# Finer steps in the hand-written engine orders of a Flowformer layer with a routed MoE behind it

## The chip, the cores and the metric

The kernel runs on one core of a Trainium2 chip. The metric is the device time of one execution in microseconds (us), lower is better. Engines are named PE (TensorE), DVE (VectorE), ACT (ScalarE), POOL (GpSimd) and SP (SyncE, which issues most transfers).

## The reference, cut to what matters

Four sequences of 1,024 tokens with 256 features pass through one decoder layer (attention without a softmax, post-norm, a GELU network of width 1,024), a norm, and then a mixture of eight experts of width 1,024, each token to one expert, with a norm behind it.

```python
q, k, v = sigmoid(heads(Wq, bq)), sigmoid(heads(Wk, bk)), heads(Wv, bv)
sink_in = normal / sum(q * cumsum(k)); src_out = normal / sum(k * cumsum(q))
cons_sink = sum(q * cumsum(k * src_out)) / normal
cons_src = exp(clip(sum(k * cumsum(q * sink_in)) / normal))
src_comp = cons_src / cumsum(cons_src) * normal
kv = cumsum(einsum('bhld,bhlm->bhldm', k, v * src_comp))
x = einsum('bhld,bhldm->bhlm', q * sink_in / normal, kv) * sigmoid(cons_sink)
h = layernorm(inputs + x @ Wo + bo)
x = layernorm(inputs + layernorm(h + gelu(h @ W1 + b1) @ W2 + b2))
e = argmax(x @ router_w.T)
out = layernorm(x + square(relu(x @ fc[e])) @ proj[e])
```

## The kernel before

All data are 32-bit floats. The 4,096 tokens are cut into eight groups of 512 (G = 8), each of four chunks of 128 (NC = 4). A group passes through five stages, each one period later than the one before it (`LAG`): stage a (projections to k, q, v, running sums, the flow's normalisers), stage p (attention inside a chunk, the running state across chunks, product with Wo, first norm), stage b (turn of the normed rows, FFN up and down), stage c (second and third norm, router), stage d (place of each row in its expert's list, scatter to DRAM). In period n the engines work on stage a of group n, p of n-1, b of n-2, c of n-3 and d of n-4. Nine periods (0 to 8) are followed by a list of its own for what is left of groups 5 to 7 and for the first six expert tiles ("the list behind period 8"), and then by a hardware loop over 33 more expert tiles of 128 rows.

There is no scheduler at run time. Each engine has a table of steps for a period (`PE_ORDER`, `DVE_ORDER`, `ACT_ORDER`, `POOL_ORDER`) and one for the list behind (`PE_LAST` and so on). `all_groups` walks them, and each step's function waits on semaphores (`ev[...]`) and issues its instructions, so an engine runs strictly in the order of its table and stands still when the next step's input is missing.

Steps that matter here, with their lines before the change: `p_share2` on PE (L479) spreads the factors `spread` over four PSUM banks, and DVE multiplies q and k by them (L1189, L1192; semaphores `qp`, `kp`) and so frees the banks for `a_proj` (L455, L461). `p_pairs` c on PE computes the scores of chunk c into the same four banks (L558) and then turns k into bank `pm` (L567); ACT copies that to `ktok` (L800), and DVE masks the scores bank by bank (L1199, `sm`). `p_mix` c on PE adds up state, masked scores and v in `pm` (L582, L590), makes the chunk's part of the state (L598), waits for ACT's copy `xat` of `pm` (L805), and multiplies by Wo (L605). Behind it DVE's `mix` updates the state (L1214, L1221), adds the residual (L1225, `r1`) and takes the mean and variance (L1205 to L1209, here "sums"). `a_dots1` is PE's dot products (L471) with DVE's reciprocal (L1128, `num`, semaphore `rden`) and product `spread` (L1121); chunk 1's scores wait for `rden`, chunk 3's for `cons` (L1160), and chunk c's for `r1` of chunk c-1. `a_comp` closes stage a (L522; DVE L1173 to L1181 and L1121). `b_turn` turns the normed rows in two halves through one bank `pb` (L617; ACT's copy L819, `n1tc`); `b_up` f and `b_down` f are the FFN's eight slices (L628, L637), with ACT's GELU between (L824). `b_add` is DVE's L1234. On POOL `p_share2` adds the bias to the residual (L946, `xb`) and makes half of the split q (L989), `b_turn` adds another bias (L951), `p_mix` and `c_sum2`, `c_sum3` take reciprocal square roots (L957), `p_norm` scales the normed rows (L973, L975, `h1b`) and `d_count` scatters the rows (L1004). The expert weights' second half (`pj`, eight transfers of 1 MB) is asked for by SP once `h1b` of group 7 is complete.

## Time and profile before

| | |
|---|---|
| Times of 3 runs | 923.64, 926.34, 928.52 us, median 926.34 |
| The profiled execution | 925.26 us, its span 923.5 us |
| PE busy | 839.4 us, 91% of the span, 6,694 matmuls |
| DVE busy | 579.0 us, 63% |
| POOL, ACT busy | 312.6 us (34%), 254.5 us (28%) |
| Chain that ended last | PE 80%, DVE 7%, all else below 4% each |
| TensorE clock, mean granted | 0.963 |

The profile's busy time counts an engine as busy while an instruction of it is under way. The time outside the span is 1.76 us. PE's share by slices of 23 us is low in the first seven slices and at 90% or more nearly everywhere behind them, where it can hide waits shorter than a microsecond; those are read from the timeline, which prints the idle time ahead of an instruction and what ended it.

### The profile page before, as it was taken

To read this page: it belongs to the slowest core of one execution; us is meant where nothing else is said; L and a number is where in the kernel's file an instruction comes from. 1 tells how busy PE (TensorE), PEld (TensorE's weight loads), DVE (VectorE), ACT (ScalarE), POOL (GpSimd) and SP (SyncE) were. 2 spreads that over 40 slices of the span, in tenths; PEclk is the share of its full clock that TensorE was granted. 3 is DMA by queue.
4 is the path that set the end of the run, shared out by engine and by line. 5 is a ranking of instruction groups with operands and counts; after the bars stand their busy time and mean duration, and the time that the engine had idled before them with its cause. 6 is when DMAs were issued, how large, how long until landed. Compare 5 with 4: busy or idle time off the path is not lost.

```text
span 923.5 us, 18688 instructions
## 1 busy us (share of the span) xinstructions
PE 839.4 (91%) x6694; PEld 635.4 (69%) x6695; DVE 579.0 (63%) x1334; ACT 254.5 (28%) x460; POOL 312.6 (34%) x425
## 2 busy tenths in 40 slices
PE   5485799999999999999999989989899999999994
PEld 3443556666666666566566666668799999999994
DVE  6867567688778788788788856545434433444432
ACT  1120241522522522522522423222112211122210
POOL 8210311522613813813713726614312222222222
PEclk9577799999999999999999999999899999999998
DMA  8999991000100200200100000794535555455540
GB/s 267 287 312 318 308 292 63 1 1 2 46 2 1 70 2 1 70 1 6 42 2 19 30 1 24 258 329 139 195 116 173 169 191 192 170 176 166 178 166 1
DMA packets 69682, 110.54 MB, mean 120 GB/s; under 512 B 5229, under 2 KB 54255, under 8 KB 69616
## 3 DMA queue, kind: packets, MB, share of 16 engines
q1 hardware_dynamic: 66208, 101.17, 35.3%
q0 software_dynamic: 3408, 8.46, 2.5%
q8 instruction: 45, 0.74, 0.4%
q14 instruction: 21, 0.17, 0.1%
HBM read 66.94 MB, written 43.58 MB: 120 GB/s over the span
## 4 chain that ended last, share of the span: by engine, by line
PE 80%; DVE 7%; SPq 3%; ACT 3%; issue 2%; DMA 2%; POOL 2%; POOLq 0%; DVEq 0%; ACTq 0%
PE bank L710 15%; PE bank L700 14%; PE bank L628 10%; PE bank L637 10%; PE bank L455 6%; PE bank L590 5%; PE bank L605 4%; PE bank L558 3%; PE bank L461 3%; SPq L383 2%; PE bank L479 2%; PE bank L582 2%; DMA pj<-in_pj 1%; ACT xat L805 1%; PE bank L567 1%
## 5 line engine op out<-in xcount | busy, mean ns | idle before, releaser
L957 POOL TENSOR_TENSOR rstd<-vare,minus_half 128x1 f32<-128x1 f32 x96 | 67.0, 700 | 330.4 <-DVE vare L1209 329.5
L700 PEld LDWEIGHTS bank<-xsT,fc 128*128 128x128 f32 x1248 | 147.7, 195 | 4.6 <-issue 2.9
L700 PE MATMUL bank<-xsT,fc 128*128 128x128 f32 x1248 | 148.8, 278 | 2.2 <-ACT xsT L843 1.7
L628 PE MATMUL bank<-n1T,w1s 128*128 128x512 f32 x256 | 122.1, 599 | 1.5 <-ACT hT L824 0.8
L637 PE MATMUL bank<-w2s,hT 128*128 128x256 f32 x512 | 122.6, 383 | 0.4 <-ACT hT L824 0.4
L637 PEld LDWEIGHTS bank<-w2s,hT 128*128 128x128 f32 x512 | 93.5, 190 | 22.1 <-issue 6.9
L850 ACT ACTIVATE relu<-bank 128x512 f32<-128x512 f32 x78 | 46.5, 597 | 207.4 <-PE bank L700 207.4
L1199 DVE TENSOR_TENSOR sm<-bank,upto 128x512 f32<-128x512 f32 x128 | 79.4, 683 | 32.0 <-PE bank L558 32.0
L710 PE MATMUL bank<-pj,act 128*128 x416 | 94.3, 380 | 1.6 <-DMA pj<-in_pj 1.6
L710 PEld LDWEIGHTS bank<-pj,act 128*128 128x128 f32 x416 | 77.0, 190 | 11.4 <-issue 2.0
L1014 POOL TENSOR_TENSOR mrstd<-mvare,minus_half 128x1 f32<-128x1 f32 x39 | 22.1, 566 | 165.3 <-DVE mvare L1370 165.3
L628 PEld LDWEIGHTS bank<-n1T,w1s 128*128 128x128 f32 x256 | 46.2, 191 | 40.8 <-issue 32.1
L455 PE MATMUL bank<-xT,wqkvo 128*128 128x512 f32 x128 | 61.5, 631 | 6.3 <-DMA xT<-in_xT 5.5
L824 ACT ACTIVATE hT<-bank,b1s 128x512 f32<-128x512 f32 x64 | 43.8, 684 | 83.2 <-PE bank L628 83.1
L1362 DVE COPY token<-xs 128x1 int32<-128x1 int32 x39 | 6.0, 154 | 93.5 <-PE bank L710 93.5
L1017 POOL DMA_INDIRECT out_rows<-y,token x39 | 40.6, 1041 | 52.2 <-DVE y L1373 50.9
L1352 DVE TENSOR_TENSOR act<-bank,relu 128x512 f32<-128x512 f32 x52 | 35.6, 689 | 32.3 <-ACT relu L850 31.5
L590 PE MATMUL bank<-sm,vpad 128*32 128x128 f32 x1024 | 46.2, 285 | 7.2 <-DVE sm L1199 7.2
L455 PEld LDWEIGHTS bank<-xT,wqkvo 128*128 128x128 f32 x128 | 25.4, 203 | 37.8 <-issue 37.8
L710 PE MATMUL bank<-pj,hT 128*128 x208 | 47.3, 380 | 1.2 <-DVE res L1363 0.9
L605 PE MATMUL bank<-wqkvo,xat 128*128 128x256 f32 x128 | 37.0, 412 | 12.0 <-ACT xat L805 12.0
L590 PEld LDWEIGHTS bank<-sm,vpad 128*32 128x32 f32 x1024 | 34.2, 112 | 18.5 <-issue 15.5
(196 smaller groups left out, 1300.8 us busy)
## 6 DMA issues: line engine op xcount, KB each, us to landing
fc<-in_fc SPq DMA_DIRECT2D x39, 1024.0 KB, 5.0
routed_rows<-empty SPq DMA_DIRECT2D x64, 520.0 KB, 9.8
pj<-in_pj SPq DMA_DIRECT2D x8, 1024.0 KB, 12.9
xs<-routed_rows SPq DMA_DIRECT2D x39, 130.0 KB, 2.0
xT<-in_xT SPq DMA_DIRECT2D x8, 512.0 KB, 5.1
x<-in_x SPq DMA_DIRECT2D x8, 512.0 KB, 4.2
wqkvo<-in_wqkvo SPq DMA_DIRECT2D x4, 256.0 KB, 4.2
w1s<-in_w SPq DMA_DIRECT2D x1, 1024.0 KB, 6.6
```

The lines of the kernel that those rows point to most:

```text
L455: last = nc.tensor.matmul(BANK4[n][:], w[:, k, chunk(m)], xT[:, half, k, :], start=(k == 0), stop=(k == KT - 1))
L590: last = nc.tensor.matmul(pm[32 * j:32 * j + 32, chunk(m)], vpad[:, half, c, 4 * m + j, 32 * e:32 * e + 32], sm[:, j, 2 * m + e, :], start ...
L605: last = nc.tensor.matmul(pa[:, 0:D], xat[:, c % 2, m, :], wo[:, m, :], start=(m == 0), stop=(m == KT - 1))
L628: last = nc.tensor.matmul(pb[:], w1[:, k, chunk(f)], n1T[:, k, :], start=(k == 0), stop=(k == KT - 1))
L637: last = nc.tensor.matmul((po0, po1)[c // 2][:, (c % 2) * D:(c % 2) * D + D], hT[:, f % 2, chunk(c)], w2[:, f, :], start=(f == 0 and c % 2 ...
L700: last = nc.tensor.matmul(h_bank[n][:, chunk(f)], fc[:, s, k, chunk(4 * n + f)], xsT[:, k, :], start=(k == 0), stop=(k == KT - 1))
L710: last = nc.tensor.matmul(o_bank[:, 0:D], actT[s][:, f, :], rows, start=(f == 0), stop=(f == FE - 1))
L824: nc.scalar.activation(hT[:, f % 2, :], pb[:], ACT.Gelu, bias=b1[:, f:f + 1])\
L850: nc.scalar.activation(relu[:, n], src[:], ACT.Relu).then_inc(M["relu"].sem, 1)
L957: nc.gpsimd.tensor_tensor(rstd[:, n, c], vare[:, n, c], minus_half[:], ALU.pow)\
L1017: nc.gpsimd.indirect_dma_start(out=out_d, out_offset=bass.IndirectOffsetOnAxis(ap=token[:, s:s + 1], axis=0), in_=y[:, s], in_offset=None, ...
L1199: nc.vector.tensor_tensor(sm[:, n], BANK4[n][:].rearrange("p (h t) -> p h t", h=4), upto[:].unsqueeze(1).broadcast_to([P, 4, P]), ALU.mult)\
```

## The change

The functions that hold two or more steps are cut. On PE the turn of k becomes a step of its own (`p_kt`), so does the product with Wo (`p_out`), and the two halves of the turn of the normed rows are `b_turn` 0 and 1. On DVE the four masks of a chunk are four steps (`p_mask` 0 to 15), and `mix` is cut into the state's update (`p_state`) and residual with sums (`p_sums`). On POOL the bias and the split of q are two steps (`p_xb`, `p_split`). All ten tables are written anew. No instruction is added or taken away, and no wait inside a step changes; only the order of steps on each engine does.

```diff
 PE_ORDER = [
...
-    ("b_turn", 0), ("p_share2", 0), ("b_up", 0), ("a_proj", 0), ("d_count", 0), ("a_proj", 1), ("a_proj", 2),
...
+    ("p_share2", 0), ("d_count", 0), ("a_proj", 0), ("b_turn", 0), ("a_proj", 1), ("b_turn", 1), ("a_proj", 2),
...
 POOL_ORDER = [
-    ("p_share2", 0), ("c_sum2", 0), ("c_sum2", 1), ("c_sum3", 0), ("c_sum2", 2), ("c_sum3", 1), ("c_sum3", 2),
-    ("p_mix", 0), ("p_mix", 1), ("c_sum2", 3), ("b_turn", 0), ("p_mix", 2), ("p_norm", 0), ("c_sum3", 3),
-    ("d_count", 0), ("p_mix", 3), ("p_norm", 1), ("p_norm", 2), ("p_norm", 3),
+    ("c_sum2", 0), ("p_split", 0), ("c_sum2", 1), ("b_turn", 0), ("p_xb", 0), ("c_sum3", 0), ("d_count", 0),
+    ("c_sum2", 2), ("c_sum3", 1), ("p_mix", 0), ("p_norm", 0), ("p_mix", 1), ("c_sum3", 2), ("c_sum2", 3),
+    ("p_mix", 2), ("p_norm", 1), ("p_norm", 2), ("c_sum3", 3), ("p_mix", 3), ("p_norm", 3),
...
+            def turn_k(g, half, c):
                 ev["xatc"].wait(pe, g, c)
...
+            def attn_out(g, half, c):
                 ev["xatc"].wait(pe, g, c + 1)
                 ev["sm"].wait(pe, g, 4 * c + 3)
...
-            def turn(g, half, _):
+            def turn(g, half, m):
                 ev["n1"].wait(pe, g, NC)
-                for m in range(KT):
-                    if m == 0:
-                        ev["gelu"].wait(pe, g - 1, FT)
-                    else:
-                        ev["n1tc"].wait(pe, g, 1)
-                    for c in range(NC):
-                        last = nc.tensor.transpose(pb[:, chunk(c)], n1[:, half, c, chunk(m)], ident[:])
-                    last.then_inc(S["n1t"], 1)
+                if m == 0:
+                    ev["gelu"].wait(pe, g - 1, FT)
+                else:
+                    ev["n1tc"].wait(pe, g, 1)
+                for c in range(NC):
+                    last = nc.tensor.transpose(pb[:, chunk(c)], n1[:, half, c, chunk(m)], ident[:])
+                last.then_inc(S["n1t"], 1)
...
-            def take_h(g, half, _):
-                for m in range(KT):
-                    ev["n1t"].wait(act, g, m + 1)
-                    nc.scalar.activation(n1T[:, m, :], pb[:], ACT.Copy).then_inc(S["n1tc"], 1)
+            def take_h(g, half, m):
+                ev["n1t"].wait(act, g, m + 1)
+                nc.scalar.activation(n1T[:, m, :], pb[:], ACT.Copy).then_inc(S["n1tc"], 1)
...
+            def mask(g, half, i):
+                c, n = i // 4, i % 4
                 ev["av"].wait(dve, g, c)
...
+            def first_sums(g, half, c):
                 ev["xb"].wait(dve, g, 1)
                 ev["wo"].wait(dve, g, c + 1)
                 ev["n1"].wait(dve, g - 1, c + 1)
```

**PE, start of a period.** The rows of PE at the end of period 2 and the start of period 3, before the change (x8 in the turn is both halves, x8 in L455 all four projections):

```order
L637 MATMUL bank<-w2s,hT 128x256 x8
L617 MATMUL bank<-ident,n 128x128 x8
L479 MATMUL bank<-spread,of_head 128x512 x4
L628 MATMUL bank<-n1T,w1s 128x512 x2
L455 MATMUL bank<-xT,wqkvo 128x512 x8
L461 MATMUL bank<-wqkvo,xT 128x256 x8
L628 MATMUL bank<-n1T,w1s 128x512 x2
L637 MATMUL bank<-w2s,hT 128x256 x4
```

And the same place after it (L482 is the share, L458 and L464 the projections, L621 the turn, L632 and L641 up and down):

```order
L641 MATMUL bank<-w2s,hT 128x256 x8
L482 MATMUL bank<-spread,of_head 128x512 x4
L458 MATMUL bank<-xT,wqkvo 128x512 x2
L621 MATMUL bank<-ident,n 128x128 x4
L458 MATMUL bank<-xT,wqkvo 128x512 x2
L621 MATMUL bank<-ident,n 128x128 x4
L458 MATMUL bank<-xT,wqkvo 128x512 x2
L632 MATMUL bank<-n1T,w1s 128x512 x2
L458 MATMUL bank<-xT,wqkvo 128x512 x2
L464 MATMUL bank<-wqkvo,xT 128x256 x8
L632 MATMUL bank<-n1T,w1s 128x512 x2
```

The turn has moved behind the share and the first projection, its halves lie one projection apart, and the first up product has moved from ahead of the projections to ahead of the last one.

**PE, middle of a period.** PE's rows from chunk 0's product with v to chunk 1's scores in period 3, before:

```order
L590 MATMUL bank<-sm,vpad 32x128 x16
L598 MATMUL bank<-vpad,ktok 32x32 x8
L605 MATMUL bank<-wqkvo,xat 128x256 x2
L651 MATMUL bank<-ident,xrow 128x128 x2
L471 MATMUL bank<-cc,head_at 32x128 x16
L658 MATMUL bank<-rw,xrT 128x8 x2
L558 MATMUL bank<-qm,kT 128x256 x8
```

And after (L594 and L602 are the former L590 and L598, L610 is Wo, L571 the turn of k, L561 the scores):

```order
L594 MATMUL bank<-sm,vpad 32x128 x16
L602 MATMUL bank<-vpad,ktok 32x32 x8
L474 MATMUL bank<-cc,head_at 32x128 x16
L610 MATMUL bank<-wqkvo,xat 128x256 x2
L655 MATMUL bank<-ident,xrow 128x128 x2
L632 MATMUL bank<-n1T,w1s 128x512 x2
L662 MATMUL bank<-rw,xrT 128x8 x2
L571 MATMUL bank<-ident,kT 128x128 x2
L561 MATMUL bank<-qm,kT 128x256 x8
```

The dot products stand between the product with v and Wo, an up product between the turn of the routed rows and the logits, and chunk 1's turn of k ahead of its scores.

**DVE, end of a period.** DVE's rows from chunk 3's state update to the routing's first row in period 3, before:

```order
L1221 TENSOR_TENSOR state<-state,sttmp 128x64
L1225 TENSOR_TENSOR r<-bank,xb 128x256
L1205 BN_STATS bst<-r 128x6
L1207 BN_AGGR mv<-bst 128x2
L1209 TENSOR_SCALAR vare<-mv 128x1
L1173 TENSOR_SCALAR den<-den 64x128
L1175 SCALAR_TENSOR_TENSOR den<-ones_t,bank,num 64x128
L1179 RECIPROCAL recip<-den 128x128
L1181 TENSOR_TENSOR comp<-recip,num 128x128
L1121 TENSOR_TENSOR spread<-comp,weight_at 128x512
L1263 TENSOR_REDUCE best<-bank 128x4
```

And after (each line number is one or two less than before):

```order
L1219 TENSOR_TENSOR state<-state,sttmp 128x64
L1172 TENSOR_SCALAR den<-den 64x128
L1174 SCALAR_TENSOR_TENSOR den<-ones_t,bank,num 64x128
L1178 RECIPROCAL recip<-den 128x128
L1180 TENSOR_TENSOR comp<-recip,num 128x128
L1120 TENSOR_TENSOR spread<-comp,weight_at 128x512
L1224 TENSOR_TENSOR r<-bank,xb 128x256
L1203 BN_STATS bst<-r 128x6
L1205 BN_AGGR mv<-bst 128x2
L1207 TENSOR_SCALAR vare<-mv 128x1
L1262 TENSOR_REDUCE best<-bank 128x4
L1264 TENSOR_TENSOR hit<-bank,best 128x32
```

The chain of `a_comp` (den to spread) now runs ahead of chunk 3's residual and sums. Besides this, `c_sum3` 0 has moved on DVE from between the running sums of `a_proj` 2 and 3 to ahead of `d_count`, and in periods 1 to 7 chunk c's sums follow the reciprocal (c = 0) or `cons` (c = 2) instead of standing ahead of them.

## Rows read from the trace of the kernel before

**Rows 1.** Stretches: start:end, length, busy us per engine, PE clock, DMA share, GB/s.
```profile
127.30:244.10 116.80, 111.18 (x1084) 73.69 (x1083) 88.83 (x177) 37.94 (x67) 34.66 (x46) 1.00 0.17 48
244.10:517.40 273.30, 261.86 (x2357) 173.81 (x2356) 222.10 (x485) 99.26 (x172) 116.11 (x149) 1.00 0.07 21
...
575.20:688.00 112.80, 102.55 (x607) 86.84 (x608) 53.65 (x170) 27.05 (x54) 42.23 (x59) 0.97 0.61 202
```

**Rows 2.** Timeline of TensorE, period 4: start, length, instruction, idle before and releaser.
```profile
244.10 0.60 PE L617 MATMUL bank<-ident,n 128*128 128x128 f32 x4
245.38 0.66 PE L617 MATMUL bank<-ident,n 128*128 128x128 f32 x4 [0.69 <-ACT n1T L819]
...
269.21 1.13 PE L605 MATMUL bank<-wqkvo,xat 128*128 128x256 f32 x4 [0.39 <-ACT xat L805]
...
272.65 1.15 PE L558 MATMUL bank<-qm,kT 32*128 32x256 f32 x16 [0.54 <-DVE num L1128]
...
312.46 0.60 PE L617 MATMUL bank<-ident,n 128*128 128x128 f32 x4
...
314.33 1.14 PE L479 MATMUL bank<-spread,of_head 32*128 32x512 f32 x8
...
319.08 1.04 PE L669 MATMUL bank<-onehot,ones 128*128 128x32 f32 x8
```

**Rows 3.** Timeline of TensorE, periods 1 and 2.
```profile
74.00 1.15 PE L558 MATMUL bank<-qm,kT 32*128 32x256 f32 x16 [1.31 <-DVE num L1128]
...
110.00 1.11 PE L617 MATMUL bank<-ident,n 128*128 128x128 f32 x4 [2.85 <-ACT n L813]
...
127.17 1.88 PE L628 MATMUL bank<-n1T,w1s 128*128 128x512 f32 x4
```

**Rows 4.** Timeline of VectorE, period 1.
```profile
73.00 0.95 DVE L1128 RECIPROCAL num<-bank 128x128 f32<-128x128 f32 x1
73.98 0.69 DVE L1121 TENSOR_TENSOR spread<-num,normal_at 128x512 f32<-128x512 f32 x1
```

**Rows 5.** Stretch after the first turn of period 2.
```profile
110.00:115.00 5.00, 4.31 (x17) 2.08 (x17) 1.34 (x2) 1.20 (x2) 4.78 (x6) 0.50 1.10 299
```

**Rows 6.** Timeline of VectorE, end of period 7.
```profile
511.54 0.23 DVE L1221 TENSOR_TENSOR state<-state,sttmp 128x64 f32<-128x64 f32 x1
512.78 0.42 DVE L1225 TENSOR_TENSOR r<-bank,xb 128x256 f32<-128x256 f32 x1 [1.01 <-PE bank L605]
...
516.15 1.10 DVE L1121 TENSOR_TENSOR spread<-comp,weight_at 128x512 f32<-128x512 f32 x1
...
518.60 1.40 DVE L1234 TENSOR_TENSOR r<-bank,h1b 128x256 f32<-128x256 f32 x4
520.52 1.29 DVE L1189 TENSOR_TENSOR qs<-bank,qT 128x512 f32<-128x512 f32 x2 [0.51 <-PE bank L479]
```

**Rows 7.** Timelines of VectorE and GpSimd, two encounters in period 5.
```profile
326.86 1.27 DVE L1084 TENSOR_TENSOR_SCAN cc<-ones_t,carry,qT 128x512 f32<-128x512 f32 x1
...
327.02 1.45 POOL L957 TENSOR_TENSOR rstd<-vare,minus_half 128x1 f32<-128x1 f32 x1 [4.43 <-DVE vare L1209]
...
364.09 2.35 POOL L951 TENSOR_TENSOR x<-x,be2s 128x1024 f32<-128x1024 f32 x1
...
365.00 1.53 DVE L1221 TENSOR_TENSOR state<-state,sttmp 128x64 f32<-128x64 f32 x1
```

**Rows 8.** Timeline of TensorE, period 8 and the list behind it.
```profile
532.54 2.44 PE L590 MATMUL bank<-sm,vpad 128*32 128x128 f32 x29 [1.90 <-DVE sm L1199]
...
603.68 1.98 PE L628 MATMUL bank<-n1T,w1s 128*128 128x512 f32 x4 [0.78 <-ACT hT L824]
...
621.14 3.71 PE L710 MATMUL bank<-pj,act 128*128 x16 [1.62 <-DMA pj<-in_pj]
...
664.32 0.41 PE L685 MATMUL bank<-ident,xs 128*128 128x128 f32 x2 [2.30 <-issue]
```

**Rows 9.** Timeline of GpSimd: the last half norm of group 7.
```profile
578.40 0.73 POOL L975 TENSOR_TENSOR h1b<-hg,be1s 128x256 f32<-128x256 f32 x1
```

More of the change, by code:

```diff
@@ L80 @@
+    ("p_kt", 1), ("p_pairs", 1), ("b_up", 3), ("p_mix", 1), ("p_out", 1), ("b_down", 2), ("a_share1", 0),
+    ("c_route", 1), ("b_up", 4), ("b_down", 3), ("p_pairs", 2), ("b_up", 5), ("b_down", 4), ("c_logit", 1),
+    ("b_down", 5), ("p_kt", 2), ("b_up", 6), ("p_mix", 2), ("a_dots2", 0), ("p_out", 2), ("c_route", 2),
+    ("p_pairs", 3), ("c_logit", 2), ("p_kt", 3), ("b_up", 7), ("p_mix", 3), ("a_comp", 0), ("p_out", 3),
+    ("b_down", 6), ("c_route", 3), ("c_logit", 3), ("b_down", 7),
 ]
 PE_LAST = [
-    ("b_turn", 7, 0), ("b_up", 7, 0), ("d_count", 5, 0), ("b_up", 7, 1), ("b_down", 7, 0), ("c_route", 6, 0),
@@ L98 @@
-    ("a_scan2", 1), ("p_pairs", 2), ("c_sum2", 3), ("p_mix", 2), ("a_dots2", 0), ("c_sum3", 3), ("p_pairs", 3),
-    ("p_mix", 3), ("a_comp", 0), ("c_choose", 0), ("b_add", 0),
+    ("p_share2", 0), ("c_sum2", 0), ("c_sum2", 1), ("c_sum3", 0), ("d_count", 0), ("a_proj", 0), ("a_proj", 1),
+    ("a_proj", 2), ("a_proj", 3), ("a_proj", 4), ("a_proj", 5), ("p_mask", 0), ("p_mask", 1), ("p_mask", 2),
+    ("p_mask", 3), ("c_sum3", 1), ("c_sum2", 2), ("p_state", 0), ("a_dots1", 0), ("p_sums", 0), ("p_mask", 4),
@@ L100 @@
+    ("p_mask", 5), ("p_mask", 6), ("p_mask", 7), ("c_sum3", 2), ("p_state", 1), ("p_sums", 1), ("a_share1", 0),
+    ("a_scan2", 0), ("a_scan2", 1), ("p_mask", 8), ("p_mask", 9), ("p_mask", 10), ("p_mask", 11), ("c_sum2", 3),
+    ("p_state", 2), ("a_dots2", 0), ("p_sums", 2), ("p_mask", 12), ("p_mask", 13), ("p_mask", 14), ("p_mask", 15),
+    ("c_sum3", 3), ("p_state", 3), ("a_comp", 0), ("p_sums", 3), ("c_choose", 0), ("b_add", 0),
 ]
 DVE_LAST = [
[1 row of a table removed]
[1 row of a table added]
     ("c_sum2", 6, 3), ("c_sum3", 6, 2), ("c_sum3", 6, 3), ("b_add", 7, 0), ("c_sum2", 7, 0), ("c_sum2", 7, 1),
[2 rows of a table removed]
@@ L117 @@
+    ("b_up", 0), ("b_up", 1), ("p_pairs", 0), ("c_row", 0), ("p_mix", 0), ("c_route", 0), ("b_up", 2), ("p_pairs", 1),
+    ("p_mix", 1), ("p_norm", 0), ("b_up", 3), ("c_row", 1), ("b_up", 4), ("b_up", 5), ("c_route", 1), ("p_norm", 1),
+    ("p_pairs", 2), ("c_row", 2), ("b_up", 6), ("p_mix", 2), ("c_route", 2), ("p_pairs", 3), ("p_norm", 2),
+    ("a_dots2", 0), ("p_mix", 3), ("c_row", 3), ("b_up", 7), ("c_route", 3), ("p_norm", 3),
 ]
 ACT_LAST = [
-    ("b_turn", 7, 0), ("b_up", 7, 0), ("b_up", 7, 1), ("c_row", 6, 0), ("b_up", 7, 2), ("c_route", 6, 0),
@@ L126 @@
-    ("m_hidden", 5, 0),
+    ("b_turn", 7, 0), ("b_turn", 7, 1), ("b_up", 7, 0), ("b_up", 7, 1), ("b_up", 7, 2), ("c_row", 6, 0),
+    ("b_up", 7, 3), ("c_route", 6, 0), ("b_up", 7, 4), ("b_up", 7, 5), ("c_row", 6, 1), ("b_up", 7, 6),
+    ("c_row", 6, 2), ("b_up", 7, 7), ("m_rows", 0, 0), ("c_route", 6, 1), ("m_hidden", 0, 0), ("c_route", 6, 2),
+    ("c_row", 6, 3), ("m_rows", 1, 0), ("c_route", 6, 3), ("m_hidden", 1, 0), ("c_row", 7, 0), ("m_rows", 2, 0),
+    ("c_route", 7, 0), ("c_row", 7, 1), ("c_route", 7, 1), ("m_hidden", 2, 0), ("c_row", 7, 2), ("m_rows", 3, 0),
@@ L1006, in scatter @@
                         in_=xrow[:, half, c, :], in_offset=None).then_inc(scattered[half], 16)
-            def start_pairs(g, half, _):
-                add_bo(g, half, 0)
-                split_q(g, half, 0)
             def store(t, s):
@@ L1022, in early_store @@
                 store(j // 3, j % 3)
-            all_groups(POOL_ORDER, POOL_LAST, {"p_share2": start_pairs, "p_mix": root1, "p_norm": scaled_h, "b_turn": add_be2,
+            all_groups(POOL_ORDER, POOL_LAST, {"p_xb": add_bo, "p_split": split_q, "p_mix": root1, "p_norm": scaled_h, "b_turn": add_be2,
                               "c_sum2": root2, "c_sum3": root3, "d_count": scatter,
@@ L1193, in scaled_q @@
                         .then_inc(S["kp"], 1)
-            def pairs(g, half, c):
+            def mask(g, half, i):
+                c, n = i // 4, i % 4
                 ev["av"].wait(dve, g, c)
-                for n in range(4):
-                    ev["s"].wait(dve, g, 4 * c + n + 1)
-                    nc.vector.tensor_tensor(sm[:, n], BANK4[n][:].rearrange("p (h t) -> p h t", h=4),
-                                            upto[:].unsqueeze(1).broadcast_to([P, 4, P]), ALU.mult)\
-                        .then_inc(S["sm"], 1)
+                ev["s"].wait(dve, g, i + 1)
+                nc.vector.tensor_tensor(sm[:, n], BANK4[n][:].rearrange("p (h t) -> p h t", h=4),
+                                        upto[:].unsqueeze(1).broadcast_to([P, 4, P]), ALU.mult).then_inc(S["sm"], 1)
             def stats(g, n, src, c):
```

49 lines of the change are left out of this document (18 added, 31 removed), and 12 rows, old and new, of tables (DVE_LAST, POOL_LAST).

## The prediction

> **What bounds the kernel now.** I read the page first: PE is busy for 839.4 of 923.5 us and makes up 80% of the chain. So I cut the span into stretches [rows 1]. From the end of period 2's projections to the start of period 4 PE is busy for 111.18 of 116.80 us, in periods 4 to 7 for 261.86 of 273.30 (11.44 us idle, 2.9 a period), in the list behind period 8 for 102.55 of 112.80. Since the change adds and removes no instruction, all it can move is PE's idle time and the clock, and the other engines only count where they end one of PE's waits. So the next view is PE's timeline of one full period, from turn to turn 244.10 to 312.46, 68.36 us [rows 2]: 0.69 us between the turn's halves (ACT copies the one bank), 0.54 ahead of chunk 1's scores (DVE's reciprocal), and four times 0.39 ahead of Wo (ACT's copy `xat`; one such row is shown). That is 2.79; a further 0.1 to 0.2 stands at the last down product. The opening has longer ones [rows 3]: 1.31 ahead of chunk 1's scores, 2.85 ahead of the first turn, and 0.69 behind it. There the granted clock is 0.50 of full speed, the 1.2 GHz level, for 5 us after PE resumes [rows 5]. Behind period 7 there are 1.90 (masks), 0.78 (two up products in a row), 1.62 (expert weights) and 2.30 (rows of the loop's first tile) [rows 8].
>
> **A full period, waits that go.** The turn's second half now has a projection before it, 1.88 us [rows 2], against 0.69: gone. Chunk 1's scores now have Wo (1.13), an up product (1.88 [rows 3]), routing rows and the turn of k between them and the dot products, over 3.4 us; DVE needs 0.95 + 0.69 for `num` and `spread` [rows 4] and 0.42 for the residual [rows 6], 2.1: the 0.54 goes. Wo of chunk 0 and 2 has dot products before it, longer than 0.39: two of the four go. Wo of chunk 1 still follows its product directly: 0.39 stays. Chunk 3 has only the one or two columns of `a_comp` between: 0.2 stays.
>
> **A full period, waits that come.** (1) Chunk 3's scores wait for `r1` of chunk 2. Before, a down product lay between Wo and them, now only a pair of turns (0.3): 0.42 and the hand-over leave 0.25. (2) Turn and logits of routed chunk 3 are now neighbours: ACT's copy takes as long as `xat`, 0.4. (3) The turn used to cover `b_add`; now share and first projection come first. DVE, end of period 7 [rows 6]: from the end of the state update (511.77) to the end of `b_add` (520.00) 8.23 us, of which 1.01 is waiting for Wo. With `a_comp` first nothing waits, so `b_add` ends at 519.0, 1.6 behind the period's end at 517.42, and the first product for `qp` (1.29 for two) ends at 2.2. PE has the share (1.07 to the next row) and the count (1.04) [rows 2] before that projection, 2.1: the wait is 0.2 with hand-over. In period 3 there is no count and no choice, `b_add` cannot start before the period's end, and 1.40 + 0.65 against 1.07 leaves 1.0.
>
> What stays is 0.39 + 0.2 + 0.25 + 0.4 + 0.2 = 1.45 of 2.87, so **1.4 us less in each of periods 4 to 7, 5.6**. In period 3 it is 2.9 to 2.2, **0.7**. In period 2 no routing exists: four times 0.39 and a wait like the 1.31 of period 1, 2.85 in all, fall to 0.39 + 0.55 + 0.25: **1.6**.
>
> **The opening.** Chunk 1's masks no longer stand behind chunk 0's sums and `num`; scores start 0.3 earlier, since `spread` (0.69) now precedes the residual, masks 0.8 earlier. In chunk 3 `cons` is no longer behind the sums: 0.4 more. At the boundary of periods 1 and 2, PE waited 2.85 for the norm and 0.69 for the copy. Now the norm has the share and a projection before it, but the share waits for `a_comp` and then `r1`, about 2.5 us behind the last Wo. So 3.5 becomes 2.6; the wait is long enough to expect the low clock again, and over the same 5 us, but with PE busy throughout it loses 0.1 more. Total to the end of period 2's projections (127.17 before): 0.8 + 0.4 + 0.9 - 0.1 = **2.0**.
>
> **Period 8 and behind.** In period 8 the first product with v waited 1.90 for masks, behind DVE's routing tables. That DVE list is the same but starts 1.0 earlier (the wait in (3)): **1.0**. In the list behind, the second turn-to-up wait (0.69) is covered by the count, the 0.78 goes since down 6 lies between up 7 and down 7 and their order alternates, the 0.56 before the first expert's up product and one of the logit waits are covered: 2.4. The 1.62 goes only if the weights come earlier. POOL finished group 7's `h1b` at 579.13 [rows 9] with three norms in a row behind a late root; two of them are now done sooner, so the request goes out some 2.4 us earlier, while the first expert's down product has moved 1.3 us later in PE's list. So it is hidden, but 1.3 of other work that filled time behind it is used up. I count **2.1** for the list. The wait of 2.30 at the loop's start stays: count 7, scatter and load follow one another as before and PE has the same products meanwhile. The loop is not touched.
>
> **Sum.** 2.0 + 1.6 + 0.7 + 5.6 + 1.0 + 2.1 = 13.0 off the profiled execution's 925.26, 912.3. The median of the runs is 1.1 above it, so I forecast **913.0** for the median.
>
> **What DVE and POOL do to each other.** [rows 7] show POOL's root beginning 0.16 behind the start of a scan and taking 1.45 instead of some 0.6, as if it stood until the scan was over; and DVE's state update, otherwise 0.23 [rows 6], taking 1.53 inside POOL's 2.35 us addition of a bias. After the change both of POOL's long additions (`b_turn`, `p_xb`) fall among DVE's four running sums of a period, 1.27 each. I price this between nothing and both additions and a root, 5.3 us, on a chain whose slack is 1.2 ahead of the fourth running sum (it waits for its projection) and 2.3 between masks and the product with v: 0 to 1.8 us a period. I take 0: DVE issues the sums back to back, and in the first encounter it was POOL that stood.
> The Trainium skill, "SBUF — State Buffer", section "SBUF: two separate sides", says that a DVE instruction with two SBUF inputs and a GpSimd instruction that reads SBUF exclude each other for the whole of an instruction, whoever starts first. Both encounters agree with that; by it the scans would be exposed, which is the first rival.
>
> **Rivals.**
> A, the additions win: if POOL gets its turn between two scans, each loses up to 2.4 us twice, the masks come late, and each of periods 2 to 7 gives back up to 1.8, 5 to 11 in all: 918 to 924. For it: the rows above; against it: the slack of 3.5 us.
> B, slower than before: DVE's chain from the state update to the first `qp` product is now unbroken and ends in PE's wait at the period's start. It starts only when ACT's exponentials are done, and ACT now has chunk 2's norm ahead of them. I reckon ACT ready 1.3 us before DVE asks. Each us by which it is later than that is one us of PE in each of six periods; at 3.5 us later the gain of 13 is eaten, at 4.5 it is 930. Against it: ACT is 28% busy and the norm's input is there 2 us behind chunk 2's residual.
> C, the order gives more: PE's wait at the first boundary stays short enough that the clock holds (2.5 us more), and the loop's start wait shrinks by part of 2.30: 907 to 910.
> D, the waits are only moved: as many small hand-overs appear elsewhere as go, 922 to 928. Against it: each was looked up in the new table.
>
> **Chances.** Forecast 0.68 (its own range 909.5 to 916.5), A 0.14, B 0.05, C 0.07, D 0.06. The range takes in C in part and most of A: 907.5 to 919.5. A measurement of this kernel tells 0.5%, 4.6 us, from nothing: faster by more than that 0.87, within 0.08, slower 0.05.
>
> **What the new profile would show.** PE's idle rows ahead of Wo halve to about 15; none ahead of the turn's second half in periods 2 to 7; a new wait on DVE's `qs` at the first projection, 0.2, in period 3 about 1.0; new waits of 0.25 on `r1` at chunk 3's scores and 0.4 on `xrT`. The period is 66.9 us. Wrong would be: a period above 67.8, running sums far above 1.27 or masks ending PE's waits (A), the exponentials ending DVE's (B), a mean clock more than 0.005 from 0.963 (C), a first expert's down product that waits over 1 us for its weights.

## The result: 919.4 us against 926.2, half of the gain forecast

The changed kernel took 919.37 us (median of 6 runs, 917.90 to 922.71), the kernel before 926.23 (6 runs, 923.64 to 928.52). The ratio is 0.9933, with a 95% interval of 0.991 to 0.996: 6.9 us faster, inside the range, where 13 was forecast. The profiled execution of the changed kernel was among its longer ones, 922.71 us with a span of 921.0. Later, in the third series of experiments, the same kernel gave 919.62 with a profiled span of 917.2; both profiles are used below, as the first and the second execution. L numbers of the changed kernel differ by a few from those of before: 561 was 558 (scores), 594 was 590 (product with v), 610 was 605 (Wo), 482 was 479 (share), 621 was 617 (turn), 1083 was 1084 (running sums), 1106 was 1107 (`vpad`, v with its bias), 954 and 949 were 951 and 946 (POOL's two additions).

I began with PE's waits, grouped by what ended them:

```profile
engine line waited for: us in total, times, longest us
PE bank L561 <- DVE vpad L1106: 9.4, 6, 1.9
...
PE bank L561 <- DVE r L1224: 5.4, 8, 1.0
...
PE bank L662 <- ACT xrT L840: 4.1, 9, 0.5
PE bank L610 <- ACT xat L809: 3.9, 11, 0.4
...
PE bank L458 <- DVE qs L1188: 2.9, 3, 1.1
```

The lower rows are foreseen: Wo waits 11 times instead of the 15 I named, `r` and `xrT` stand where they should (`r` at 0.56 to 0.59 in periods 3 to 7 instead of 0.25), `qs` is up to 1.1 in period 3. The first row is not foreseen at all. Six times PE stands ahead of scores until v has its bias. One of them, 0.94 in period 1, is in the kernel before too; the other five, 8.4 us together, are one in each of periods 3 to 7. To see why v is late I read the timelines of the three engines in period 7, which begins with the share at 445.63 (columns: start, time, engine, line, operation, out<-in; in brackets the idle time before it and what ended it). The first four rows are DVE's, then three of POOL, then PE's:

```profile
453.97 2.45 DVE L1083 TENSOR_TENSOR_SCAN cc<-ones_t,carry,kT 128x512 f32<-128x512 f32 x2
456.34 6.54 DVE L1083 TENSOR_TENSOR_SCAN cc<-ones_t,carry,qT 128x512 f32<-128x512 f32 x2
462.80 1.39 DVE L1106 TENSOR_TENSOR vpad<-bank,bvs 128x256 f32<-128x256 f32 x4
...
455.58 3.00 POOL L954 TENSOR_TENSOR x<-x,be2s 128x1024 f32<-128x1024 f32 x1
458.53 3.27 POOL L949 TENSOR_TENSOR xb<-x,bos 128x1024 f32<-128x1024 f32 x1
461.75 1.47 POOL L960 TENSOR_TENSOR rstd<-vare,minus_half 128x1 f32<-128x1 f32 x1
...
460.88 1.88 PE L632 MATMUL bank<-n1T,w1s 128*128 128x512 f32 x4
464.65 1.94 PE L561 MATMUL bank<-qm,kT 32*128 32x256 f32 x16 [1.89 <-DVE vpad L1106]
```

The two running sums of k take 2.45, the two of q 6.54. The second sum of k ends at 456.42. POOL's first addition is recorded from 455.58; if it stood until 456.42, then both additions and both sums of q did their work in the 6.46 us from there to 462.88, when the last sum ends. Two additions alone (2.35 in [rows 7]) and two sums alone (1.27) make 7.24. So the four ran one after another but for 0.2 to 0.3 us at each hand-over, each engine standing while the other worked, in turns: addition, sum, addition, sum. A pair of them takes 3.3 where its parts alone make 3.62. All sums of q over the kernel, by duration, say that this is the rule:

```profile
L1083 DVE TENSOR_TENSOR_SCAN cc<-ones_t,qT x8: 1191/2263/3309, 14.7 to 391.2; 128x512 f32<-128x512 f32 x8
L1083 DVE TENSOR_TENSOR_SCAN cc<-ones_t,carry,qT x8: 1283/3302/3311, 58.5 to 459.6; 128x512 f32<-128x512 f32 x8
```

(ns of the shortest, the median and the longest.) It is rival A's mechanism, but with the wait at another place than I had looked.

The table puts the stages beside the forecast. Each begins with PE's first instruction of it (before: the turn; after: the share). The last column is a kernel from the experiments, both additions taken away from the sums, profiled on the chip of the second execution.

| stage | before | forecast gain | gain, first execution | gain, second | gain without the collision |
|---|---|---|---|---|---|
| to the start of period 3 | 176.92 | 3.6 | 4.4 | 6.0 | 3.0 |
| period 3 | 67.18 | 0.7 | 0.1 | 0.1 | 1.0 |
| periods 4 to 7 | 273.3 | 5.6 | -2.2 | -0.5 | 7.9 |
| period 8 | 57.8 | 1.0 | -3.6 | -3.6 | -0.7 |
| list behind | 89.1 | 2.1 | 3.5 | 2.7 | 4.2 |
| loop to the end | 259.2 | 0 | 0.3 | 1.6 | 1.6 |
| span | 923.5 | 13.0 | 2.5 | 6.3 | 17.0 |

Everything was gained ahead of period 3 and behind period 8, and given back between. The stretches of the first execution, for comparison with [rows 1]:

```profile
172.55:239.60 67.05, 63.42 (x574) 1.00 0.05 17
239.60:515.08 275.48, 262.45 (x2358) 0.99 0.07 21
515.08:576.48 61.40, 56.30 (x492) 0.92 0.03 10
576.48:662.09 85.61, 78.92 (x467) 1.00 0.71 234
```

(Columns: stretch, us, PE busy, count, granted clock, DMA share, GB/s.) Periods 4 to 7 hold 13.0 us of idle PE; before it was 11.44.

Period 8 lost 3.6 in either execution. In the first its PE timeline begins, behind the share:

```profile
516.15 0.41 PE L670 MATMUL bank<-onehot,before 128*128 128x40 f32 x2
516.39 1.04 PE L673 MATMUL bank<-onehot,ones 128*128 128x32 f32 x8
517.29 0.64 PE L621 MATMUL bank<-ident,n 128*128 128x128 f32 x4
519.20 0.83 PE L621 MATMUL bank<-ident,n 128*128 128x128 f32 x4 [1.27 <-ACT n1T L822]
520.72 3.78 PE L632 MATMUL bank<-n1T,w1s 128*128 128x512 f32 x4 [0.69 <-ACT n1T L822]
525.27 3.78 PE L632 MATMUL bank<-n1T,w1s 128*128 128x512 f32 x4 [0.78 <-ACT hT L827]
```

Stage a has no group left in period 8, so no projection lies between the turn's halves: 2.74 us of waits, and up products of 3.78 where [rows 3] have 1.88, the 1.2 GHz level. The wait of 1.90 for masks [rows 8] is not to be seen. The second execution, where the clock stayed up longer, took the same 61.40 us, and there the masks' wait is back. DVE's rows, then POOL's, then PE's (the period begins at 511.82):

```profile
520.88 2.38 DVE L1318 CAST filled<-count_i 128x8 f32<-128x8 int32 x1
523.30 2.27 DVE L1301 TENSOR_TENSOR_SCAN end<-ones,filled 128x8 f32<-128x8 f32 x1
...
520.89 2.34 POOL L954 TENSOR_TENSOR x<-x,be2s 128x1024 f32<-128x1024 f32 x1
523.20 2.33 POOL L949 TENSOR_TENSOR xb<-x,bos 128x1024 f32<-128x1024 f32 x1
...
530.19 2.44 PE L594 MATMUL bank<-sm,vpad 128*32 128x128 f32 x29 [1.07 <-DVE sm L1198]
```

A cast and a running sum of eight columns, which in the kernel without the collision take 0.17 each,

```profile
514.75 0.17 DVE L1301 TENSOR_TENSOR_SCAN end<-ones,filled 128x8 f32<-128x8 f32 x1
```

stand here for the whole of an addition each: the routing tables are 4.3 us later, and the masks behind them 4.4. In period 8 the collision is with them. Both executions took 61.40 us, one with slow products and no wait for masks, one with the wait, so here the clock only decided in which form PE met the delay.

### The profile page after: what moved, and what is told of

The parts are those of the page before. It is cut to its first block, busy times and chain, and to the rows that moved or that the text cites. A ratio compares the mean times of both kernels' runs of the same rounds, so it can differ in the third digit from the quotient of the medians.

```text
span 921.0 us, 18787 instructions
## 1 busy us (share of the span) xinstructions
PE 840.8 (91%) x6694; PEld 637.6 (69%) x6695; DVE 593.7 (64%) x1334; ACT 253.6 (28%) x459; POOL 317.0 (34%) x425
## 4 chain that ended last, share of the span: by engine, by line
PE 81%; DVE 12%; issue 4%; ACT 2%; DMA 1%; POOL 0%; POOLq 0%; DVEq 0%; SPq 0%; ACTq 0%
PE bank L704 16%; PE bank L714 15%; PE bank L641 12%; PE bank L632 11%; PE bank L594 4%; DVE cc L1083 4%; PE bank L458 4%; PE bank L561 4%; PE bank L610 3%; PE bank L474 2%; PE bank L586 2%; PE bank L662 2%; PE bank L464 2%; PE bank L482 1%; PE bank L689 1%
## 5 line engine op out<-in xcount | busy, mean ns | idle before, releaser
L960 POOL TENSOR_TENSOR rstd<-vare,minus_half 128x1 f32<-128x1 f32 x96 | 64.8, 676 | 274.4 <-DVE vare L1207 274.3
L632 PE MATMUL bank<-n1T,w1s 128*128 128x512 f32 x256 | 125.9, 615 | 2.2 <-ACT hT L827 1.6
L641 PE MATMUL bank<-w2s,hT 128*128 128x256 f32 x512 | 124.6, 388 | 0.0
L641 PEld LDWEIGHTS bank<-w2s,hT 128*128 128x128 f32 x512 | 96.8, 193 | 23.5 <-issue 11.9
L632 PEld LDWEIGHTS bank<-n1T,w1s 128*128 128x128 f32 x256 | 46.0, 194 | 45.7 <-issue 38.8
L458 PE MATMUL bank<-xT,wqkvo 128*128 128x512 f32 x128 | 66.7, 656 | 9.1 <-DMA xT<-in_xT 6.2
L561 PE MATMUL bank<-qm,kT 32*128 32x256 f32 x512 | 38.7, 418 | 17.7 <-DVE vpad L1106 9.4
L458 PEld LDWEIGHTS bank<-xT,wqkvo 128*128 128x128 f32 x128 | 25.2, 210 | 36.7 <-issue 36.7
L594 PE MATMUL bank<-sm,vpad 128*32 128x128 f32 x1024 | 43.9, 282 | 5.7 <-DVE sm L1198 5.7
L561 PEld LDWEIGHTS bank<-qm,kT 32*128 32x128 f32 x512 | 25.1, 193 | 31.4 <-issue 27.5
```

What stands on the lines that cost most here:

```text
L458: last = nc.tensor.matmul(BANK4[n][:], w[:, k, chunk(m)], xT[:, half, k, :], start=(k == 0), stop=(k == KT - 1))
L561: last = nc.tensor.matmul(BANK4[i][:, m * 2 * P:(m + 1) * 2 * P], kT[rows, half, m, chunk(c)], qm[rows, :, m, chunk(c)], start=True, stop= ...
L594: last = nc.tensor.matmul(pm[32 * j:32 * j + 32, chunk(m)], vpad[:, half, c, 4 * m + j, 32 * e:32 * e + 32], sm[:, j, 2 * m + e, :], start ...
L632: last = nc.tensor.matmul(pb[:], w1[:, k, chunk(f)], n1T[:, k, :], start=(k == 0), stop=(k == KT - 1))
L641: last = nc.tensor.matmul((po0, po1)[c // 2][:, (c % 2) * D:(c % 2) * D + D], hT[:, f % 2, chunk(c)], w2[:, f, :], start=(f == 0 and c % 2 ...
L960: nc.gpsimd.tensor_tensor(rstd[:, n, c], vare[:, n, c], minus_half[:], ALU.pow)\
```

## Experiments

Each kernel was timed against the kernel before on its chip. There were three series. In the first the kernel before took 926.77 us (13 runs), in the third 925.98 (11 runs). In the second it took 949.88 (945.68 to 954.42, 11 runs), for a reason that I could not find: there is no profile of it, and its mean granted clock, 0.950 to 0.958 against 0.961 to 0.966 in the other two, is lower but was not followed up. Kernels of that series are therefore compared with one another. Their control is the kernel with only `p_xb` moved away (909.52, below), for the one with both away was not run there. Where a kernel of that series has both away, `b_turn` is thus a second difference from its control; the medians of both away in the other two series, 909.17 and 909.78, lie beside it. Where an expectation names a theory by a letter only, L is the collision between POOL's long additions and the running sums, and C what the start of period 8 and the clock there cost. All edits are to tables of the changed kernel, unless said otherwise.

**Both additions away from the sums.** On POOL `p_xb` goes first in the period and `b_turn` behind the second norm's last root.

```diff
 POOL_ORDER = [
-    ("c_sum2", 0), ("p_split", 0), ("c_sum2", 1), ("b_turn", 0), ("p_xb", 0), ("c_sum3", 0), ("d_count", 0),
+    ("p_xb", 0), ("c_sum2", 0), ("p_split", 0), ("c_sum2", 1), ("c_sum3", 0), ("d_count", 0),
...
-    ("p_mix", 2), ("p_norm", 1), ("p_norm", 2), ("c_sum3", 3), ("p_mix", 3), ("p_norm", 3),
+    ("b_turn", 0), ("p_mix", 2), ("p_norm", 1), ("p_norm", 2), ("c_sum3", 3), ("p_mix", 3), ("p_norm", 3),
```

> The changed kernel with POOL's two long additions away from DVE's running sums: `p_xb` first in a period, `b_turn` behind `c_sum2` 3, all else as in the change. Theory L (the additions and the running sums exclude each other, v comes late, and chunk 0's scores wait for it): the running sums of q go back from 3.3 to 1.3 us, the waits of 1.1 to 1.9 us ahead of chunk 0's scores in periods 3 to 7 (8.4 in all) go, and with them the two short stretches of low clock behind such waits; 908 to 912 us. Rival T (v is late because DVE as a whole has too much ahead of the scores, with `c_sum3` 0 moved ahead of the running sums): waits stay above 1 us, time within 2 us of the change's 919.4.

Measured: 909.17 us (904.7 to 910.83, 6 runs), 0.980 of before (0.978 to 0.983), 10.2 below the changed kernel. All sums of q lie between 1.20 and 1.29 again.

The edit also costs something, ahead of period 1. With `p_xb` first in POOL's list, the addition for group 0 runs as early as period 0, and there it makes another instruction of DVE stand. The first row is from the second profile of this kernel, the other from the kernel before, which has the same addition there:

```profile
26.26 2.34 DVE L1120 TENSOR_TENSOR spread<-num,normal_at 128x512 f32<-128x512 f32 x1
```

```profile
26.04 2.45 DVE L1054 COPY weight_at<-normal_at 64x512 f32<-64x512 f32 x1
```

They take 0.69 and 0.42 in the changed kernel, whose `p_xb` comes at 52.98. In the first case PE's wait ahead of the share in period 0 is 3.56 instead of 1.91, in the second its wait ahead of the dot products behind it is 4.62 instead of 2.88. The old kernel with nothing but POOL's additions moved (below) has 2.88 too. So the changed kernel gained 1.7 us in period 0 by a move of `p_xb` that was not made for it, and this edit gives 1.65 of it back.

**Period 8 started differently.** On PE the turn's halves are put around the share in period 8 alone, ACT's copies ahead of its half of the split.

```diff
+PE_START8 = [("b_turn", 0), ("p_share2", 0), ("b_turn", 1), ("d_count", 0)]
+ACT_START8 = [("b_turn", 0), ("b_turn", 1), ("p_share2", 0)]
...
+        if n == G and order is PE_ORDER:
+            order = PE_START8 + [step for step in order if step not in PE_START8]
+        if n == G and order is ACT_ORDER:
+            order = ACT_START8 + [step for step in order if step not in ACT_START8]
```

> The changed kernel with another start of period 8 alone: on PE turn 0, share, turn 1, count; on ACT both copies of the turn ahead of the split of q. Theory C (in period 8 three waits in 5 us, 1.27, 0.69 and 0.78, bring TensorE's clock down for 10 us): two of the three waits go, the clock stays high through period 8, and the time falls by 1.3 us of waits plus up to 5 us where the clock had fallen: 913 to 917. Rival R (the clock falls in some executions by itself, whatever PE waits for): only the waits go, 917.5 to 918.5, and the profile still shows a low stretch in period 8.

Measured: 922.31 us (916.51 to 925.34, 8 runs), no gain, and above what either theory expected. PE's timeline shows the turn's waits gone and another come:

```profile
532.66 1.74 PE L600 MATMUL bank<-sm,vpad 128*32 128x128 f32 x10 [3.95 <-DVE sm L1204]
```

PE waits 3.95 for the masks: DVE, with its routing tables and the additions among them, sets this part of period 8, and what PE does before only decides where it waits. The period took 62.2 us instead of 61.4.

**Both edits.**

> Both edits together. Theories L and C: the gains add up, 903 to 909 us, mean granted clock at or above that of the kernel before. T and R: 916 to 919.

Measured: 910.93 us (909.08 to 912.77, 5 runs), as with the additions' edit alone; the two gains do not add up. Its period 8 took 57.3 us against 58.5 in the profiled executions: with the collision gone, the other start is worth 1.2 there, too little to be seen in the medians.

**The collision put into the kernel before.** The old kernel, in which only POOL's additions are placed among the sums of k:

```diff
-            def start_pairs(g, half, _):
-                add_bo(g, half, 0)
-                split_q(g, half, 0)
...
+    ("p_share2", 0), ("c_sum2", 0), ("c_sum2", 1), ("b_turn", 0), ("p_xb", 0), ("c_sum3", 0), ("c_sum2", 2),
```

> The kernel before with one edit: POOL's two long additions put between its roots `c_sum2` 1 and `c_sum3` 0, beside DVE's running sums, all other tables as they were. Theory L: the running sums of q lengthen to 3.3 us here too, chunk 0's scores wait 1 to 2 us more in periods 3 to 7, and the kernel before becomes slower by 5 to 12 us: 931 to 938. Rival T: a change of POOL's order alone costs under 1 us.

Measured: 937.59 us (937.27 to 939.42, 4 runs), 1.012 of before (1.010 to 1.013), 10.8 slower. The waits again name `vpad`, and in period 8 the masks:

```profile
PE bank L590 <- DVE sm L1195: 11.9, 3, 5.9
...
PE bank L558 <- DVE vpad L1103: 4.3, 6, 1.0
```

The same two instructions cost 10 us in either order of everything else, but not in the same places. Here a running sum of k and a cast stand (3.3 and 2.2 us), hardly ever a sum of q, and the waits for `vpad` are 0.4 to 1.0 instead of the 1 to 2 expected. Period 3 is 1.8 longer, periods 4 to 7 are 5.1, period 8 is 4.6, with a wait of 5.91 for masks, and the list behind 2.9.

**Only one of the additions away.** If each addition costs in proportion, half of the 10 us should come back; if there is a slack that holds one of them, nearly all. First only `p_xb` moved away, `b_turn` left among the sums (second series):

> The changed kernel with one of POOL's two long additions moved back: `p_xb` first in a period, `b_turn` still beside DVE's running sums. Theory L, each addition delays one running sum by 2.0 us: the wait ahead of chunk 0's scores, 1.1 to 1.9 us with both, was what was left of 4 us of delay above the slack, so with one it falls to 0 and the time is close to that of both moved back (909.2): 908 to 912. Rival: the cost is shared in equal parts, 914.

Measured: 909.52 us (906.43 to 912.89, 6 runs). Then only `b_turn` moved away (third series, with the next two kernels as controls):

```diff
 POOL_ORDER = [
-    ("c_sum2", 0), ("p_split", 0), ("c_sum2", 1), ("b_turn", 0), ("p_xb", 0), ("c_sum3", 0), ("d_count", 0),
+    ("c_sum2", 0), ("p_split", 0), ("c_sum2", 1), ("p_xb", 0), ("c_sum3", 0), ("d_count", 0),
...
-    ("p_mix", 2), ("p_norm", 1), ("p_norm", 2), ("c_sum3", 3), ("p_mix", 3), ("p_norm", 3),
+    ("b_turn", 0), ("p_mix", 2), ("p_norm", 1), ("p_norm", 2), ("c_sum3", 3), ("p_mix", 3), ("p_norm", 3),
```

> The changed kernel with only the addition of b_turn taken away from the running sums; p_xb stays among them. Theory of a slack that one addition fits into: scores wait for v only once DVE is late by more than about 1 us, and one addition makes it late by 2.4 to 3, partly ahead of a sum that waits for its projection anyway. So one addition costs little: 909 to 912, and its mirror image (only p_xb away) was 909.5. Rival, that p_xb is the costly one, for it comes last, where the slack is used up: 915 to 919.

> The changed kernel as it is, once more, as a control for the three beside it: 919 +- 3 us whatever the theory. What differs between theories is read in the others against this one.

> The changed kernel with both of POOL's long additions away from the running sums, once more, as a control on this chip. The collision theory: 909 +- 3, some 10 us below the changed kernel. If the 10 us were a matter of that one chip, the two would lie within 3 us here.

Measured: 906.52 us (905.83 to 909.49, 5 runs); the changed kernel 919.62 (918.38 to 921.64, 6 runs), with both additions away 909.78 (908.24 to 910.33, 5 runs). So the 10 us stand on this chip too, and either addition alone costs nothing that the medians show. The rival, that `p_xb` is the costly one, falls. By stages it is less even. Periods 4 to 7 take 265.40 with only `b_turn` away and 264.58 with only `p_xb` away, against 265.37 with both: there one addition is free. Period 8 takes 61.24 and 60.25 against 58.48. Its cast still stands for 2.38 us and the masks start 2.5 and 2.3 later, but PE does not wait for them, and its granted clock is low for longer, so how much of this is the addition's is not shown. With only `b_turn` away period 3 starts at 169.36 against 173.94, since `p_xb` is not in period 0; this hides what period 8 lost. The slack can be read from the same place in period 7. With both away (period from 439.32), DVE's rows and then PE's:

```profile
450.04 1.26 DVE L1083 TENSOR_TENSOR_SCAN cc<-ones_t,carry,qT 128x512 f32<-128x512 f32 x1
452.05 1.28 DVE L1083 TENSOR_TENSOR_SCAN cc<-ones_t,carry,qT 128x512 f32<-128x512 f32 x1 [0.75 <-ACT qT L781]
453.25 0.73 DVE L1106 TENSOR_TENSOR vpad<-bank,bvs 128x256 f32<-128x256 f32 x2
454.85 0.76 DVE L1106 TENSOR_TENSOR vpad<-bank,bvs 128x256 f32<-128x256 f32 x2 [0.87 <-PE bank L464]
...
454.58 1.88 PE L632 MATMUL bank<-n1T,w1s 128*128 128x512 f32 x4
456.39 1.15 PE L561 MATMUL bank<-qm,kT 32*128 32x256 f32 x16
```

With only `b_turn` away (period from 434.77), DVE, POOL, PE:

```profile
445.49 4.48 DVE L1083 TENSOR_TENSOR_SCAN cc<-ones_t,carry,qT 128x512 f32<-128x512 f32 x2
449.90 1.39 DVE L1106 TENSOR_TENSOR vpad<-bank,bvs 128x256 f32<-128x256 f32 x4
...
444.73 2.99 POOL L949 TENSOR_TENSOR xb<-x,bos 128x1024 f32<-128x1024 f32 x1
...
451.84 1.15 PE L561 MATMUL bank<-qm,kT 32*128 32x256 f32 x16
```

Counted from the period's start, the sums end at 14.0 with both away, at 15.2 with one among them, at 17.25 with two. DVE had 0.87 of waiting for the product that gives v, and v was ready 0.8 before PE asked, of which 0.46 is needed to hand it over (v is complete at 464.19 in the changed kernel, and the scores start at 464.65). One addition, 1.2 us later, is just swallowed by that. Two, 3.3 later, leave 1.9: the scores start at 17.07, 17.07 and 19.02.

**The dot products put back behind Wo.** Both additions away, and `a_dots1`, `a_dots2`, `a_comp` behind `p_out` on PE again (second series, to be compared with 909.5).

```diff
-("a_dots1", 0), ("p_out", 0)
+("p_out", 0), ("a_dots1", 0)
...
-("a_comp", 0), ("p_out", 3)
+("p_out", 3), ("a_comp", 0)
```

> The kernel with both additions moved back, and the dot products and `a_comp` on PE put behind the product with Wo again, as before the change. The prediction's step (dot products ahead of Wo cover a wait of 0.39): two waits of 0.39 and 0.2 come back in each of periods 1 to 7, about 1.0 a period, less where chunk 3's scores wait for `cons` anyway: 4 to 7 us slower than 909.2, 913 to 916. Rival: the cover is worth nothing since chunk 1's and 3's scores then wait as much less: within 2 us of 909.2.

Measured: 925.90 us (923.68 to 928.82, 6 runs), 16.4 above its control and 16.1 above both additions away in the third series: far more than the 4 to 7 that I expected. Wo waits 32 times again, and the scores behind it wait longer for `r`:

```profile
PE bank L610 <- ACT xat L809: 11.9, 32, 0.4
PE bank L561 <- DVE r L1224: 9.7, 9, 2.0
```

These two rows are 12.2 us above those of the control (3.9 and 5.5). Against the profile with both additions away the opening is 7.6 us longer, period 3 is 2.2 and periods 4 to 7 are 7.7 (68.3 a period instead of 66.3). Of the steps put back one by one this one costs the most. The other engines' lists stay in the new order, so 16 us is what its loss costs here, not what it brought by itself. Why the opening loses 7.6 was not followed up.

**The turn's halves put together.** First both halves behind the first projection (second series):

```diff
-("a_proj", 0), ("b_turn", 0), ("a_proj", 1), ("b_turn", 1), ("a_proj", 2),
+("a_proj", 0), ("b_turn", 0), ("b_turn", 1), ("a_proj", 1), ("a_proj", 2),
```

> The kernel with both additions moved back, and the two halves of the turn put side by side on PE and ACT, behind the first projection. The prediction's step: 0.69 us comes back in each of periods 2 to 7, 4.1 us: 913. Rival: DVE or ACT sets the pace there, less than 1.5 us.

Measured: 919.34 us (916.1 to 921.66, 6 runs), 9.8 above its control. It asked the wrong question: in ACT's list the load of a function table (1.28 us) and a copy of k (0.69) come just ahead of the turn's first copy, so the half waits 1.3 to 1.5 instead of 0.69. So again with the halves ahead of the first projection and ACT's copies first in its list (third series):

```diff
-("d_count", 0), ("a_proj", 0), ("b_turn", 0), ("a_proj", 1), ("b_turn", 1), ("a_proj", 2),
+("d_count", 0), ("b_turn", 0), ("b_turn", 1), ("a_proj", 0), ("a_proj", 1), ("a_proj", 2),
...
-("p_share2", 0), ("b_turn", 0), ("a_proj", 0), ("b_turn", 1), ("a_proj", 1)
+("b_turn", 0), ("b_turn", 1), ("p_share2", 0), ("a_proj", 0), ("a_proj", 1)
```

> Both additions away from the running sums, and the two halves of the turn directly behind one another, right behind the count and ahead of the first projection, with ACT's two copies first in its list (no load of a function table between them, which the other kernel with whole turns had). If the halves' separation is worth what the kernel before showed, 0.69 us a period in periods 2 to 8: 4 to 5 us above the control, 913 to 915. If the wait for DVE's product of q, behind the share, had been costing the same time anyway in periods 2 and 3, 1 to 2 us less than that: 911 to 913.

Measured: 913.40 us (912.43 to 914.43, 4 runs), 3.6 above its control of 909.78; the wait is in its place:

```profile
380.87 0.63 PE L621 MATMUL bank<-ident,n 128*128 128x128 f32 x4 [0.78 <-ACT n1T L822]
```

Periods 4 to 7 took 268.84 against 265.37, 0.87 more each, for a printed wait of 0.78. The printed wait is not quite the whole of it (see below).

**The opening filled.** Both additions away, and about 90 useless products into a bank that is free in periods 0 to 2, placed ahead of PE's waits there, so that PE stands less (second series). The work is extra; the output is computed as before.

```diff
+FILL = {
+    (0, "a_dots1", 0): 10, (0, "a_share1", 0): 6, (0, "a_dots2", 0): 14, (0, "a_comp", 0): 9,
...
+                if order is PE_ORDER and (n, name, i) in FILL:
+                    steps["fill"](FILL[n, name, i])
```

> The kernel with both additions moved back, and in periods 0 to 2 some 90 matmuls without use (two columns blocks of Wk into a bank that the FFN's down product takes later) put ahead of the steps on which PE waits, sized to fit into the waits at full clock; the output is unchanged. If waits are what brings the clock down in the opening, the low stretches of 34, 10 and 3 us shrink to below 15 in all and the time falls by 6 to 12 us net of what the filling costs: 898 to 904. If not, the time rises by 3 to 10 us since the filling at the low clock takes twice as long as the waits.

Measured: 904.54 us (902.14 to 906.13, 6 runs), 5.0 below its control, a little above the 898 to 904 expected. The stretches of the opening, filled:

```profile
26.00:78.00 52.00, 44.74 (x396) 0.90 1.07 300
78.00:124.00 46.00, 39.49 (x353) 0.96 1.09 300
```

and with the additions away only:

```profile
26.00:78.00 52.00, 35.93 (x259) 0.71 1.08 326
78.00:124.00 46.00, 31.95 (x304) 0.85 1.10 331
```

The granted clock is 0.90 and 0.96 instead of 0.71 and 0.85. So the waits of the opening cost twice, by themselves and by the slower products behind them. It is the fastest kernel of the study, 0.952 of before on its chip, though that ratio is flattered by the 949.88; against the 926 of the other chips it would be 0.977.

## Where the prediction failed and where it held

**The step that failed** is the price of the collision: "I price this between nothing and both additions and a root ... I take 0: DVE issues the sums back to back, and in the first encounter it was POOL that stood." The runs show that neither engine wins. They take turns, and both stand: two sums of 1.27 became 6.54. What the collision cost is measured three times: 10.2 and 9.8 us by taking it out of the changed kernel, 10.8 by putting it into the old one; with half of it left in, the full periods lose nothing. In the stages, against the kernel of the last column, it is 0.9 in period 3, 8.5 (second execution) or 10.1 (first) in periods 4 to 7, and 2.9 in period 8. The opening goes the other way by 3.0 in the second execution, 1.65 of it by the early `p_xb` in period 0, so the 10 us are a balance.

The Trainium skill, "SBUF — State Buffer", section "SBUF: two separate sides", says that such a pair of instructions holds the port one at a time and whole, whoever starts first. The trace agrees, but for some 0.25 at each hand-over: four instructions that take 7.24 alone took 6.46. By that rule the sums were exposed; I had quoted it and decided against it. That the two lists take strict turns is what the trace adds.

**The slack was looked up at the wrong consumer.** I counted 1.2 ahead of the fourth sum and 2.3 between the masks and the product with v. The first is 0.75 here, and the second is never reached: DVE's list has v's bias behind the sums and ahead of the masks, and PE wants v for chunk 0's scores, a step that I had not followed back. It had 0.8 to spare, 0.46 of it for the hand-over, and 0.87 in front of it.

**The waits of a full period were nearly right, their worth too small.** Without the collision the printed waits of period 5 are 0.35 (Wo), 0.87 (`r`) and 0.47 (`xrT`), 1.7 against my 1.45: Wo of chunk 3 and `qs` have none, `r` has 0.6 more. Yet a period of 4 to 7 shrank by 2.0, not 1.4. The windows split it (periods 4 to 7, additions away):

```profile
240.12:505.49 265.37, 258.86 (x2358) 1.00 0.07 21
```

Idle time went from 11.44 to 6.51, 1.2 a period as forecast, but busy time went from 261.86 to 258.86 too, with the same matmuls. Neighbouring rows of PE overlap when it does not stand (in period 8 above 516.15 + 0.41 is 0.17 behind the next start, 516.39); the ends are modelled by the profile. My reading is that a wait breaks that overlap: three or four waits a period are gone here for 0.75 us of busy time, up to 0.2 each. The halves put together point the same way, by less: 0.87 for a printed 0.78. No run separates this from what the new order of PE's rows does by itself. Forecast 5.6, measured 7.9.

**The opening** gave 4.4, 6.0 and 3.0 in three executions for a forecast of 3.6. That the number is near is in part luck. At the boundary of periods 1 and 2 the waits are 2.48 and 0.90 in place of 2.85 and 0.69, 0.2 us less where 0.9 was forecast; the second is for `qs`, which I had expected only from period 3 on. What made up for it is period 0, where I had counted nothing: there the wait of 4.62 fell to 2.88, since `p_xb` no longer meets DVE.

**Period 8** was forecast at +1.0 and gave -0.7 without the collision, -3.6 with it. I said that the turn's second half waits for nothing "in periods 2 to 7" and did not ask what period 8 then does; its ACT copy now stands behind the split of q. The masks' wait that I wanted to shorten went by DVE's list: "the same but starts 1.0 earlier", I wrote, and passed over that POOL's additions had been moved beside it as well. Of the 4.6 us between forecast and result 2.9 are the collision.

**The list behind** was forecast at 2.1 and gave 3.5, 2.7 and 4.2. The wait for expert weights is gone, as allowed for; some 2.2 us came before the first expert's turn (34.0 to 31.8), as forecast. The loop's first tile still waits, 2.89 and 2.03. What makes up the rest of the difference was not tested. A slip in the sum is of no weight: 912.3 and 1.1 are 913.4, not 913.0.

**Rivals.** A was right in its mechanism, in its sum ("5 to 11 in all", measured 10) and in its time (918 to 924), and had a chance of 0.14 where the chip's rows, both of them encounters in which one engine stood for the whole of the other's instruction, spoke for it. It was hidden in the median by the other terms' being larger: 17 gained, 10 lost. B (late exponentials) is not seen, since `qs` ends no wait of PE in periods 4 to 7. C is not seen: at the first boundary the clock fell in every execution (0.50 from 110 to 112 in the first), though for some 3.3 us instead of 5 by the windows' means (my estimate), and the loop's first tile still waited. Only with the opening filled did the clock there rise. D is refuted: with the additions away the moved waits are fewer, and the time is 909. Of the signs of being wrong, those of A both showed: a period of 68.9 (first) and 68.5 (second) against 67.8, and sums of 3.3; the mean clock was 0.956 in the first execution, more than 0.005 off, and 0.964 in the second.

## What to carry to other kernels

When an engine's long instruction is moved beside another engine's list, and the trace holds even one encounter in which either of them stood, price it as if they ran one after the other, and then find the first consumer of what comes late, not the one that the change is about. Whether it costs is a threshold: here in a full period one addition was free, and the second cost some 2 us a period. Before a reordered table is accepted, walk the first and last periods, in which some steps are empty: what covers a wait may not be there, and a step without work to wait for runs a period early, as `p_xb` did, into whatever is on the other engine then.
